# A dense product moved to the loop's end, an unbroken ring of banks, bf16 prefix sums, a 128-row gates' product, and a second DMA issuer for the queries

## The chip, the cores and the metric

One NeuronCore of a Trainium2 chip runs the whole kernel. The metric is the device time of one execution in microseconds. Three runs of the kernel before are shown, and one profiled execution.

## What is computed

Eight batches of 512 tokens with 128 features go through two layers:

```python
x = L0_attn_x                                   # (8, 512, 128)
xn = layernorm(x)
x = x + L0_attn(xn) + L0_ffn(xn)
xn = layernorm(x)
x = x + L1_attn(xn) + L1_ffn(xn)
```

L0_attn is a causal linear attention with Taylor features (16 heads of width 8) beside an attention with a sliding window of 64, both put through Wout. L0_ffn has four layers: `silu(x w1) * (x w2)`, two dense layers h1 and h2 of 512 to 512 with gelu, and w3 of 512 to 128. L1_attn is a causal softmax attention. L1_ffn sends each token to its best 2 of 8 experts: softmax gates of the two best logits, expert e computes `gelu(x W1[e] + b1[e]) W2[e] + b2[e]`, and the results are summed by gate.

## The kernel before, in words

The kernel is written per engine, with an order set out by hand and semaphores between engines. A **batch** goes through four stages on TensorE: `linear_stage` (linear scores of this batch, between them the causal maxima of the previous batch), `causal_stage` (causal scores of the previous batch, sliding maxima of this), `slide_stage` (sliding scores of this batch, projections and the first FFN layer of the next) and `dense_stage` (the FFN's h1 and h2 of the next batch; `mixed_first`, which ends layer 0 of this batch; then the second layernorm, keys k2, queries q2, values v2 and the router's logits of this batch). An opening prepares batch 0, the first batch is written out, batches 1 to 6 run in a loop on every engine (`Fori`, line 898 on TensorE, 1059 on ScalarE, 1613 on VectorE), the last is written out, and a tail finishes its causal attention. Behind the tail, 78 expert tiles are worked through.

**The ring of banks.** Every product that another engine evacuates is a *unit*. `units_of` lists a part's units in TensorE's order, and `PLACE` gives unit n the bank n mod 7. TensorE may begin a unit when its bank's previous unit has been *taken* (`to_bank`, line 521). Each part starts at bank 0 again. The loop's part has 234 units, so its last ones (xnT2, v2, logits) lie in banks 0, 1 and 2, and the first linear products of the next turn follow in the same banks. `first` has 145 units, `last` 213.

**What crosses the joint between two batches.** On TensorE the loop's turn ends with xnT2, v2 and logits. The next turn begins with linear products (six, of which four come before `prefix`), then `h2_3`, four more linear products, `third_layer` (w3), two more, and then the causal maxima, which wait for the second queries (`slots_q2`). `h2_3` is the fourth quarter of the dense layer h2, whose inputs `hidden_b` were ready long before. `prefix` (lines 656 and 659) sums `picks`, the one-hot choices of experts, over the tokens before each: one product with the strict triangle `before_p` and four with `ones`, all fp32. VectorE takes the logits, shifts them (`shift_logits`), takes v2 and then ranks the experts (`choose_experts`) and writes `picks`. In the next turn it places the rows, waits for `third_layer` to add it up in `xs`, and runs through the causal maxima.

**Queues.** ScalarE evacuates k2 and q2 as high parts (`split_hi`), VectorE as low parts (`split_lo`). SyncE (SP) sends them to scratch memory in DRAM (`split_and_send`: two copies of the high part, one of the low part; first k2, then q2) and fetches them back in another layout (`fetch_sent`), with a wait for the complete sends before each fetch. After q2's fetch has landed it fetches q1 of the next batch. ScalarE issues DMAs only at the opening, 21 later loads, b2's among them.

**mixed_causal** (`mix_causal`, lines 631 and 632) ends layer 1's attention: for each of four token tiles `gatesT` (8 rows) times `b2` (8 rows) and, on the same sum, the attention's 128 rows times wo1. Both are fp32, two passes each.

## Time and profile before

| | us |
|---|---|
| median of 3 runs | 1498.56 |
| lowest and highest | 1495.23, 1499.37 |
| the profiled execution | 1501.17 |
| its span, first to last instruction | 1499.3 |
| TensorE busy (share of the span) | 1330.5 (89%) |
| VectorE, ScalarE, GpSimd busy | 817.6, 707.5, 603.3 |
| mean granted TensorE clock | 0.934 |

The span is the stretch in which all rows below lie; 1.9 us of the profiled execution lie around it. In the rows PE is TensorE, PEld its weight loads, DVE VectorE, ACT ScalarE, SP SyncE; a "q" behind an engine's name marks its sequencer or its DMA issues. An fp32 product appears as two passes, so its count is doubled. "Idle before" names what released the engine; "issue" is idle time without a releaser in the trace. PEclk is the granted share of TensorE's full clock.

### The profile page before, as it was taken

How to read it: one execution, taken by the hardware profiler on the slowest of the kernel's cores; microseconds unless marked ns; L12 is line 12 of the kernel's file. 1: busy time of each engine (PE TensorE's matmuls, PEld its weight loads, DVE VectorE, ACT ScalarE, POOL GpSimd, SP SyncE). 2: the span in 40 equal slices, each digit the busy share in tenths (PEclk: the TensorE clock that was granted, in tenths of full speed). 3: DMA queues.
4: the chain of work that ended last, by engine and by line, in shares of the span. 5: the costliest groups of instructions: out<-in, count | busy, mean ns of one | idle time of the engine just before them, and what ended most of it. 6: DMA issues, size and time to landing. Idle time of an engine off the chain costs nothing.

```text
span 1499.3 us, 28932 instructions
## 1 busy us (share of the span) xinstructions
PE 1330.5 (89%) x9122; PEld 917.4 (61%) x9122; DVE 817.6 (55%) x3372; ACT 707.5 (47%) x1511; POOL 603.3 (40%) x791
## 2 busy tenths in 40 slices
PE   5979999989998999989998999899989965679997
PEld 2545567656664666466656665566566743459997
DVE  3064377537753676367635753486357545436654
ACT  2435247524761466246623662366235610437765
POOL 6123334323441334143414342343243435228787
PEclk9988999999999899999998999899999975789999
DMA  9203310331023202330233022402240025014343
GB/s 263 79 2 97 94 58 9 104 101 54 8 84 95 77 9 79 83 95 10 79 76 102 10 79 50 126 11 72 57 123 13 3 70 179 7 31 66 57 65 47
DMA packets 82246, 102.07 MB, mean 68 GB/s; under 512 B 12472, under 2 KB 43104, under 8 KB 82016
## 3 DMA queue, kind: packets, MB, share of 16 engines
q1 hardware_dynamic: 63616, 86.53, 20.9%
q0 software_dynamic: 14304, 10.61, 4.5%
q10 hardware_dynamic: 4176, 3.01, 0.7%
q8 instruction: 84, 1.38, 0.4%
q14 instruction: 66, 0.54, 0.1%
HBM read 55.44 MB, written 46.37 MB: 68 GB/s over the span
## 4 chain that ended last, share of the span: by engine, by line
PE 61%; issue 14%; DVE 11%; POOL 4%; DMA 3%; ACT 2%; SPq 2%; ACTq 1%; another core or an unknown queue 1%; POOLq 0%; DVEq 0%
PE bank L552 16%; PE bank L545 16%; PE heads L609 11%; PE bank L534 6%; PE bank L530 3%; POOL out L1146 3%; DVE hrow L1284 2%; PE bank L649 2%; DVE hT_s L1284 2%; DVE xnT_s L1284 2%; SPq L425 1%; PE bank L539 1%; DVE mx_c L1284 1%; ACT probs L926 1%; ACTq L1049 1%
## 5 line engine op out<-in xcount | busy, mean ns | idle before, releaser
L926 ACT ACTIVATE probs<-bank 128x512 f32<-128x512 f32 (+2 forms) x896 | 442.5, 574 | 421.8 <-PE bank L552 419.2
L552 PE MATMUL bank<-K,Q 128*128 128x192 f32 (+4 forms) x1024 | 237.0, 323 | 37.8 <-DVE mx_c L1284 12.7
L1084 POOL TENSOR_SCALAR_AFFINE_SELECT probs<-probs 128x384 f32<-128x384 f32 x256 | 127.8, 523 | 325.4 <-ACT probs L926 299.7
L552 PE MATMUL bank<-Q,K 128*128 128x192 f32 (+4 forms) x1024 | 216.9, 328 | 16.1 <-DMA Q<-mrow_c 9.8
L552 PEld LDWEIGHTS bank<-K,Q 128*128 128x128 f32 x1024 | 172.3, 197 | 81.1 <-DVE mx_c L1284 35.1
L609 PE MATMUL heads<-probs,V 128*9 128x192 f32 (+4 forms) x3072 | 205.3, 410 | 15.4 <-DVE probs L1333 5.5
L552 PEld LDWEIGHTS bank<-Q,K 128*128 128x128 f32 x1024 | 155.3, 201 | 46.5 <-issue 24.0
L552 PE MATMUL bank<-QM,K 128*128 128x512 f32 (+3 forms) x512 | 141.9, 366 | 29.1 <-issue 18.9
L609 PEld LDWEIGHTS heads<-probs,V 128*9 128x9 f32 x3072 | 77.6, 93 | 132.7 <-issue 90.4
L1146 POOL DMA_INDIRECT out<-h1T_s x78 | 123.3, 1581 | 52.2 <-ACT h1T_s L1038 27.7
L916 ACT ACTIVATE probs<-bank,sh_s 128x512 f32<-128x512 f32 x64 | 44.0, 688 | 202.6 <-PE bank L545 202.6
L545 PE MATMUL bank<-probs,h2T_s 128*128 128x512 f32 x256 | 127.9, 643 | 4.8 <-ACT probs L916 4.8
L552 PEld LDWEIGHTS bank<-QM,K 128*128 128x128 f32 x512 | 87.2, 201 | 54.7 <-issue 24.1
L1030 ACT ACTIVATE h2T_s<-bank,h1T_s 128x128 f32<-128x128 f32 x312 | 89.2, 368 | 60.9 <-PE bank L859 48.0
L545 PE MATMUL bank<-probs,h1T_s 128*128 128x512 f32 x256 | 115.2, 594 | 1.1 <-DVE probs L1452 1.1
L1105 POOL TENSOR_TENSOR rs<-pw,half_neg 128x4 f32<-128x4 f32 x32 | 32.3, 1020 | 203.8 <-DVE pw L1246 203.8
L1097 POOL TENSOR_SCALAR_AFFINE_SELECT probs<-probs 128x512 f32<-128x512 f32 x64 | 54.9, 858 | 141.5 <-ACT probs L926 141.4
L1130 POOL DMA_INDIRECT sorted_rows<-rows,slot_i x64 | 63.6, 993 | 104.8 <-DVE mx_c L1284 86.1
L1313 DVE COPY ot<-heads 128x512 f32<-128x512 f32 x64 | 44.2, 690 | 101.0 <-PE heads L609 101.0
L545 PEld LDWEIGHTS bank<-probs,h2T_s 128*128 128x128 f32 x256 | 52.2, 211 | 61.6 <-issue 60.9
L859 PE MATMUL bank<-h1T_s,w_in 128*128 128x128 f32 x624 | 83.9, 278 | 0.0
L867 PE MATMUL bank<-w_out,h2T_s 128*128 128x128 f32 x624 | 82.5, 275 | 0.3 <-ACT h2T_s L1030 0.3
(188 smaller groups left out, 2090.3 us busy)
## 6 DMA issues: line engine op xcount, KB each, us to landing
Q<-slots_of_q SPq DMA_DIRECT2D x16, 1024.0 KB, 7.9
slots_of_q<-Q SPq DMA_DIRECT2D x48, 256.0 KB, 3.9
K<-slots_of_k SPq DMA_DIRECT2D x64, 192.0 KB
QM<-slots_of_qm SPq DMA_DIRECT2D x8, 1024.0 KB, 9.2
slots_of_k<-QM SPq DMA_DIRECT2D x24, 256.0 KB, 4.1
slots_of_qm<-Q SPq DMA_DIRECT2D x24, 256.0 KB, 4.3
slots_of_k<-Q SPq DMA_DIRECT2D x24, 256.0 KB, 3.0
h1T_s<-sorted_rows SPq DMA_DIRECT2D x78, 65.0 KB
```

The costliest lines, as they stand in the source:

```text
L534: pe.matmul(to_bank(run, unit)[:, :], w, x, start=True, stop=True).then_inc(full_sem(run, unit), 1)
L545: mm = pe.matmul(to[:, :], w[:, k, c * P:(c + 1) * P], src[k], start=(k == 0), stop=(k == FC - 1))
L552: mm = pe.matmul(to[:, at:at + right.shape[1]], left, right, start=True, stop=True, skip_group_check=True)
L609: mm = pe.matmul(heads[ROWS * i:ROWS * i + D + 1, P * j:P * j + widths[j]], V[:, j, HG * g + i, :], slot_of(kind, 2 * g + i // 2)[:, at:at ...
L859: mm = pe.matmul(tile_hidden_bank(i)[:, c * P:(c + 1) * P], w_in[:, i % WB, c * P:(c + 1) * P], tile_xT[:, i % 2, :], start=True, stop=True)
L867: mm = pe.matmul(tile_out_bank(i), tile_hidden[i % 2][:, c * P:(c + 1) * P], w_out[:, i % WB, c * P:(c + 1) * P], start=c == 0, stop=c == ...
L926: return act.activation(to, bank, func, scale=scale, bias=bias).then_inc(taken_sem(run, unit), 1)
L1030: last = act.activation(tile_hidden[i % 2][:, c * P:(c + 1) * P], tile_hidden_bank(i)[:, c * P:(c + 1) * P], ACT.Gelu, bias=tile_b1[:, i % ...
L1084: pool.affine_select(out=three, in_=three, compare_op=ALU.is_ge, fill=0.0, base=0, pattern=[[0, 3], [1, P]], channel_multiplier=-1)
L1130: pool.indirect_dma_start(out=sorted_rows, out_offset=bass.IndirectOffsetOnAxis(ap=slot_i[:, n:n + 1], axis=0), in_=rows[:, n // K2, n % K ...
L1146: pool.indirect_dma_start(out=out.rearrange("b t d -> (b t) d"), out_offset=bass.IndirectOffsetOnAxis(ap=tile_rows[:, i % XB, P + 1:P + 2] ...
L1284: last = dve.tensor_tensor_reduce(beside[:, at:at + n], bank_of(run, unit)[:, at:at + n], mask, 1.0, NEG, ALU.add, ALU.max, mx[:, to:to + 1])
```

## The change

Five things are changed at once. `h2_3` of the next batch is computed at the end of `dense_stage`, behind logits, and no longer in the next linear stage; its gelu is at the end of ScalarE's turn, which then raises a new semaphore `hidden_ready`, and `third_layer` waits for that and comes after the sixth linear product in place of the tenth. `places_of` skips banks at one unit in the middle of a part (h1_1, or cols2 in the last part), so that each part that has one ends on bank 6 and the ring goes on unbroken at its end. `picks`, `before_p` and `ones` become bf16. `gatesT` and `b2` get 128 rows, of which 120 are zero; GpSimd clears both at the start and b2 is loaded as the last of ScalarE's opening loads, after that clearing. q2 is sent by ScalarE's queue, right behind its own high part. Besides, VectorE takes v2 before it takes the logits.

```diff
@@ linear_order
-        units += linear(m) + (["prefix"] if m == 3 and before else []) + (["h2_3"] if m == 5 else []) + (["third_layer"] if m == 9 else [])
+        units += linear(m) + (["prefix"] if m == 3 and before else []) + (["third_layer"] if m == 5 else [])
@@ dense_order
     units += ["hT2", "k2", "q2", "xnT2", "v2", "logits"] if this else []
+    units += ["h2_3"] if after else []
@@
-PLACE = {part: {u: (n % BANKS, n // BANKS) for n, u in enumerate(units)} for part, units in UNITS.items()}
+def places_of(units):
+
+    at, done, place = 0, [0] * BANKS, {}
+    passed = "h1_1" if "h1_1" in units else f"cols{SLIDE}"
+    for unit in units:
+        at += -len(units) % BANKS if unit == passed else 0
+        place[unit] = at % BANKS, done[at % BANKS]
+        done[at % BANKS] += 1
+        at += 1
+    return place
+
+
+PLACE = {part: places_of(units) for part, units in UNITS.items()}
@@ build
-        b1, b2 = sb("b1_s", [P, E * FC]), sb("b2_s", [E, P])
+        b1, b2 = sb("b1_s", [P, E * FC]), sb("b2_s", [P, P])
-        gatesT = sb("gatesT_s", [E, T])
+        gatesT = sb("gatesT_s", [P, T])
-        picks, place = sb("picks", [P, NT + 1, K2 * E]), sb("place", [P, NT, K2 * E])
+        picks, place = sb("picks", [P, NT + 1, K2 * E], BF16), sb("place", [P, NT, K2 * E])
-        before_p, ones = sb("before_p", [P, P]), sb("ones", [P, P])
+        before_p, ones = sb("before_p", [P, P], BF16), sb("ones", [P, P], BF16)
@@ sync: body
                     split_and_send(run, (b, 0), "k2")
-                    split_and_send(run, (b, 0), "q2")
@@ tensor
             def third_layer(run):
-                wait_taken(run, f"h2_{FC - 1}")
+                pe.wait_ge(S["hidden_ready"], due("hidden_ready", (run[1], 0), 1))
@@ tensor: linear_stage
                     if m == 5:
-                        dense(run, "h2_3", h2T, hidden_b, 3)
-                    if m == 9:
                         if not before:
@@ tensor: dense_stage
                     project_rows(run, "logits", xnT, wgT[:, :], E)
+                if after:
+                    dense(run, "h2_3", h2T, hidden_b, 3)
@@ scalar: linear_stage
-                    if n == 5:
-                        gelu(run, "h2_3", hidden_c[3], sh2[:, 3:4])
@@ scalar: dense_stage
                     split_hi(run, now, "q2", bq1[:, 0:1])
+
+                    view = scratch["q2"].rearrange("h (s d) t -> s h d t", d=D)
+                    high, low = parts_of["q2"]
+                    act.wait_ge(S["hi_q2"], due("hi_q2", now, 1))
+                    act.sem_inc(S["unread"], 1)
+                    for s in (0, 1):
+                        act.dma_start(view[s], high.bitcast(F32)).then_inc(S["sent_q2"], 16)
+                    act.wait_ge(taken_sem(run, "q2"), taken_at(run, "q2"))
+                    act.sem_inc(S["unread"], 1)
+                    act.dma_start(view[2], low.bitcast(F32)).then_inc(S["sent_q2"], 16)
                 if after:
                     gelu(run, "h2_2", hidden_c[2], sh2[:, 2:3])
+                    gelu(run, "h2_3", hidden_c[3], sh2[:, 3:4])
+                    act.wait_ge(taken_sem(run, "h2_3"), taken_at(run, "h2_3"))
+                    act.sem_inc(S["hidden_ready"], 1)
@@ scalar: opening loads
+            act.wait_ge(S["cleared"], 1)
+            act.dma_start(b2[0:E, :], dram["b2"]).then_inc(S["later_weights"], 16)
@@ gpsimd
+            pool.memset(b2[:, :], 0.0)
+            pool.memset(gatesT[:, :], 0.0)
             pool.memset(half_neg[:, :], -0.5).then_inc(S["cleared"], 1)
@@ vector
-                take(run, "gatesT", gatesT[:, :], lambda x: x[0:E, :])
+                take(run, "gatesT", gatesT[0:E, :], lambda x: x[0:E, :])
@@ vector: dense_stage
                     take(run, "xnT2", xnT[:, :])
-                    take(run, "logits", lg[:, :, :], lambda x: x[:, 0:NT * E].rearrange("p (t e) -> p t e", e=E))
-                    shift_logits(run, now)
                     dve.wait_ge(full_sem(run, "v2"), full_at(run, "v2"))
...
+                    take(run, "logits", lg[:, :, :], lambda x: x[:, 0:NT * E].rearrange("p (t e) -> p t e", e=E))
+                    shift_logits(run, now)
                     choose_experts(now)
```

## Rows read from the trace of the kernel before

**Rows 1.** The page's busy time, share and instructions of each engine.

```profile
PE 1330.5 (89%) x9122; PEld 917.4 (61%) x9122; DVE 817.6 (55%) x3372; ACT 707.5 (47%) x1511; POOL 603.3 (40%) x791
```

**Rows 2.** Timeline of TensorE: start, us, engine, line, operation, out<-in, shapes, xcount [idle <-releaser].

```profile
481.26 1.06 PE L539 MATMUL bank<-wgT_s,xnT_s 128*128 128x8 f32 x8
486.34 2.17 PE L552 MATMUL bank<-QM,K 128*128 128x512 f32 x6 [4.02 <-issue]
488.31 0.66 PE L656 MATMUL bank<-picks,before_p 128*128 128x80 f32 x2
...
490.41 1.20 PE L552 MATMUL bank<-QM,K 128*128 128x256 f32 x3
491.41 5.87 PE L545 MATMUL bank<-probs,h2T_s 128*128 128x512 f32 x8
...
498.16 3.73 PE L649 MATMUL bank<-w3T_s,probs 128*128 128x128 f32 x32
...
502.20 0.68 PE L552 MATMUL bank<-K,Q 128*128 128x512 f32 x3
```

**Rows 3.** Waits of TensorE, 310 to 960 us: who <- whom: us, times, longest.

```profile
PE bank L552 <- issue: 18.9, 5, 4.0
```

**Rows 4.** Line 898, 470 to 490 us: duration ns min/median/max, first and last start.

```profile
L898 PEldq COMPARE_BRANCH  x1: 4616/4616/4616, 481.4 to 481.4; - x1
```

**Rows 5.** Timeline of VectorE, 470 to 495 us.

```profile
470.70 0.69 DVE L1555 TENSOR_TENSOR x<-bank,xs 128x512 f32<-128x512 f32 x1 [5.30 <-PE bank L641]
...
493.23 0.23 DVE L1360 TENSOR_TENSOR place<-bank,base 128x64 f32<-128x64 f32 x1 [7.29 <-issue]
```

**Rows 6.** Timeline of ScalarE, 479.9 to 481 us.

```profile
480.00 0.69 ACT L916 ACTIVATE probs<-bank,sh_s 128x512 f32<-128x512 f32 x1 [0.17 <-PE bank L545]
```

**Rows 7.** Line 1059 (ScalarE's loop), columns as in rows 4.

```profile
L1059 ACTq FUSED_REGOPS  x1: 50/50/50, 480.3 to 480.3; - x1
```

**Rows 8.** Windows: stretch, its us, busy (instructions) by engine, PEclk, DMA share, GB/s.

```profile
485.80:496.00 10.20, 9.66 (x25) 6.80 (x26) 1.05 (x7) 3.15 (x6) 5.46 (x7) 0.50 0.74 180
```

**Rows 9.** Timeline of TensorE, 0 to 95 us (the opening and the first batch).

```profile
59.31 2.07 PE L552 MATMUL bank<-QM,K 128*128 128x512 f32 x9
61.22 3.60 PE L545 MATMUL bank<-probs,h2T_s 128*128 128x512 f32 x8
```

**Rows 10.** Timeline of TensorE, 330 to 347 us (another joint with a branch).

```profile
331.87 1.97 PE L552 MATMUL bank<-QM,K 128*128 128x512 f32 x6 [4.04 <-issue]
...
346.36 0.68 PE L552 MATMUL bank<-K,Q 128*128 128x512 f32 x3
```

**Rows 11.** Timeline of TensorE, 468 to 471 us (mixed_first).

```profile
468.71 1.95 PE L641 MATMUL bank<-wout_s,attnT 128*128 128x128 f32 x16
```

**Rows 12.** Timeline of TensorE, 176 to 195 us (the loop's entry).

```profile
176.56 1.06 PE L539 MATMUL bank<-wgT_s,xnT_s 128*128 128x8 f32 x8
...
181.29 0.45 PE L656 MATMUL bank<-picks,before_p 128*128 128x80 f32 x2 [1.84 <-DVE picks L1352]
...
194.84 0.45 PE L552 MATMUL bank<-K,Q 128*128 128x512 f32 x1
```

**Rows 13.** Timeline of the SyncE queue, 478 to 496.5 us.

```profile
480.87 1.99 SPq L399 DMA_DIRECT2D slots_of_q<-Q  x3
...
487.19 8.79 SPq L408 DMA_DIRECT2D Q<-slots_of_q  x2
```

**Rows 14.** Windows, columns as in rows 8.

```profile
482.00:484.00 2.00, 0.32 (x3) 0.23 (x3) 1.57 (x6) 0.00 (x0) 0.93 (x1) 1.00 0.94 287
```

**Rows 15.** Timeline of TensorE, 589.3 to 592.9 us (mixed_causal).

```profile
589.45 0.48 PE L631 MATMUL bank<-b_s,gatesT_s 8*128 8x128 f32 x2
589.87 0.49 PE L632 MATMUL bank<-wo_s,attnT 128*128 128x128 f32 x2
```

**Rows 16.** Windows behind a mixed_causal, columns as in rows 8.

```profile
895.00:905.50 10.50, 10.50 (x74) 8.18 (x76) 3.83 (x7) 5.07 (x12) 3.71 (x6) 0.52 0.09 27
```

**Rows 17.** Timeline of the ScalarE queue, 14 to 17.5 us (an opening load).

```profile
14.69 2.38 ACTq L1049 DMA_DIRECT2D earlier_s<-in_earlier  x1
```

More of the change, by code:

```diff
@@ L180 @@
 UNITS = {part: units_of(*has) for part, has in PARTS.items()}
-PLACE = {part: {u: (n % BANKS, n // BANKS) for n, u in enumerate(units)} for part, units in UNITS.items()}
+def places_of(units):
[8 more added lines that the diff above has]
+PLACE = {part: places_of(units) for part, units in UNITS.items()}
 def units_in(part, bank):
-    return len(range(bank, len(UNITS[part]), BANKS))
+    return sum(at == bank for at, _ in PLACE[part].values())
 def units_before(part, bank):
@@ L308, in build @@
             "x1_ready": 1, "shifted": 1, "exped": 1, "gated": 1, "picked": 1, "placed": 1, "rows_filled": 2, "gates_filled": 1,
-            "token_laps": 1, "third_added": 1, "rows_sent": NT * K2 * 16,
+            "token_laps": 1, "hidden_ready": 1, "third_added": 1, "rows_sent": NT * K2 * 16,
             "routing_set": 0, "after_sent": 0, "pads_sent": 0, "pads_counted": 0, "list_laps": 0, "lists_ready": 0,
@@ L1045, in _ @@
                            (bv1[:, :], dram["bv1"].partition_broadcast(P)), (wgT[:, :], dram["wgT"]), (b1[:, :], dram["b1"]),
-                           (bo1[:, :], dram["bo1"].partition_broadcast(P)), (earlier[:, :], dram["earlier"]), (b2[:, :], dram["b2"]),
-                           (wo1[:, :], dram["wo1"])]
+                           (bo1[:, :], dram["bo1"].partition_broadcast(P)), (earlier[:, :], dram["earlier"]), (wo1[:, :], dram["wo1"])]
             for dst, src in later_loads:
                 act.dma_start(dst, src).then_inc(S["later_weights"], 16)
-            assert len(later_loads) == LATER_LOADS
+            act.wait_ge(S["cleared"], 1)
+            act.dma_start(b2[0:E, :], dram["b2"]).then_inc(S["later_weights"], 16)
+            assert len(later_loads) + 1 == LATER_LOADS
             act.wait_ge(S["setup_done"], 1)
```

## The prediction

> **What bounds the kernel now.** I read the page's engine shares first. TensorE is busy for 1330.5 of 1499.3 us [rows 1], so the kernel gets faster where TensorE has less to issue, idles less or runs more often at its upper clock. Next I read TensorE's timeline from one batch to the next. The router's projection (logits) ends at 482.32 (481.26 + 1.06), then TensorE idles 4.02 us and resumes at 486.34 [rows 2]. That idle has no releaser ("issue"); the waits add five of them up to 18.9 us [rows 3]. The sequencer's own row names it: the loop's backward branch begins at 481.4 and takes 4.616 us [rows 4]. Logits had begun only just before it and ran on to 482.32 meanwhile, so queued work goes on under the branch. At the same joint VectorE stands still for 7.29 us with no releaser [rows 5], and ScalarE hardly at all: its last gelu starts at 480.00, and the first register instruction of the next turn is at 480.3 [rows 6, 7]. After the gap TensorE's granted clock is 0.50, that is 1.2 GHz, for 10.2 us [rows 8].
>
> The change touches seven joints between batches: five with a taken branch, and the entry and the exit of the loop, which have none. It also touches the gates' product of each of eight batches, and the last batch's tail. I measure a joint from x1, the residual sum on VectorE (470.70 here [rows 5]), to the first product of the causal maxima, "bank<-K,Q" (502.20 here [rows 2]).
>
> **h2_3 before the branch.** It leaves the lower clock, where it takes 5.87 us [rows 2], and goes behind logits, where it should take the 3.60 us of the upper clock [rows 9]. It lies in the bank of h2_2, so it waits for that gelu, which I put at 482.6 (below): 0.2 us of idle. It starts at 482.55, and what follows could go at 486.0. Like logits it is eight passes, so I let the branch begin as soon as the wait clears: 482.6 + 4.6 + 0.3 = 487.5 against 486.34 before. That is **1.1 us later**, but with h2_3 done, and with 1.4 us of idle instead of 4.0. Behind it, new: six linear products 1.91 us (59.31 to 61.22 [rows 9]), the prefix 0.45, the third layer 3.5 (its row's 3.73 less the overlap with its follower [rows 2]), six linear products more 2.0: **7.85 us** to the causal maxima. Old: 486.34 to 502.20, 15.9 us here. Another such joint takes 331.87 to 346.36, 14.5 [rows 10]; three more are like that one. Net 4 x (14.5 - 7.85 - 1.1) + (15.9 - 7.85 - 1.1) = 22.2 + 6.95 = **29.2 us**. Of this the prefix and the clock are a part.
>
> **Prefix in bf16.** Five fp32 products take ten passes, 488.31 to 490.41, 2.1 us [rows 2] at the lower clock. In bf16 each is one pass. No row has such a pass; the nearest are fp32 passes of 128 columns, 16 in 1.95 us, 0.12 each [rows 11], and double that at the lower clock: five take 0.6 to 1.2 us by them. The prefix has only 240 columns of the 640 in five such passes, which would be 0.22. Between 0.22 and 1.2 I take 0.45, near the rows' upper-clock end. VectorE's writing of picks as bf16 may cost or save a tenth of a microsecond; at a branch nobody waits for it. At the joints without one TensorE waits 1.84 us for picks [rows 12]; h2_3 now covers that.
>
> **Joints without a branch.** Old: logits end at 177.6, maxima at 194.84, 17.2 us [rows 12]. New: 0.2 + 3.45 + 7.85 = 11.5. But the second queries must have landed: their fetch starts at 487.19, and the next one, which waits for them, has been issued at 495.98 [rows 13], so they land at 495.5 or so, x1 + 24.8. With the 0.5 us of the next part this bounds the joint from below at x1 + 24.3. That is 4.5 us won instead of 5.7 at the entry, a little more at the exit: **9.4 us** for both. At a branch my sum gives 495.2, x1 + 24.5: the queries are just in time there, and no more can be had.
>
> **q2 sent by ScalarE's queue.** SP issues the sends from 480.87, behind the keys, 1.99 us for three [rows 13]. ScalarE has finished the high part before its gelu at 480.00 [rows 6], so the first send can go 0.9 us earlier. The DMA engines' share is already 0.94 over 482 to 484 [rows 14], so early queries delay keys: the gain at the fetch is between 0 and 0.9, and lies near the saturated end, 0.5 at most. The price is on ScalarE: three issues of 0.66 (SP's) and two waits ahead of the gelu of h2_2, which moves from 480.00 to 481.9 and is done at 482.6. Queued behind it are h2_3's gelu and ScalarE's branch; TensorE waits 0.2 us for it, counted above. ScalarE is next needed at 488.3. SP passes on to the fetch of the keys, which waits for their landing as before. In the tail, where the maxima wait for the queries alone, **0.5 us** is gained.
>
> **Gates' product over 128 rows.** Pairs of passes of 8 rows and of 128 rows alternate, a pair every 0.42 us (589.45, 589.87), so 3.4 us for 16 passes [rows 15]. Mixed_first is 16 passes of the same size, all of 128 rows, in 1.95 us [rows 11]. Eight times 1.45 is **11.6 us**, on the path since TensorE has no idle around it. The clock fell behind three of these eight: once to 0.52 for 10.5 us, 5 us lost [rows 16], twice for about 3.3 us, 1.6 each. The passes over 8 rows come right before it fell; I credit half of 8.2, **4 us**, with bounds of 0 and 8.2.
> The Trainium skill (TensorE: Matmul & The Clock Gate, "Step-by-step: what each phase is for") says that the time of a weight load goes by its columns and "row count K doesn't matter here". By that rule alone this part would bring nothing; the two rows speak against it.
>
> **Ring, memsets, b2.** The skip now stands at h1_1, which comes onto the last slide products' banks, long read by then: 0 us, and an exponential (0.6 us) where one isn't. In exchange the first linear products no longer follow v2 and logits in their banks. Two memsets and a later load of b2 lie beside the opening's loads: 0 us, bound 1.
>
> **Clock and VectorE.** The clock fell at all seven joints ([rows 8] is one of them), each time after 1.3 to 4 us of idle with small products around it. A dense h2_3 and 1.4 us of idle is better but not clean. I charge half the joints with a short stretch of 3.4 us at half speed: 7 x 0.5 x 1.7 = **-6**. VectorE, back at about 492.6, has placed rows by 493.8; the third layer ends at 494.2. Its refetch under full DMA queues may run late: **-3**.
>
> **Sum.** 29.2 + 9.4 + 0.5 + 11.6 + 4 - 6 - 3 = 45.7. The profiled execution took 1501.17 us (span 1499.3), 2.6 above the median of the three runs: 1501.2 - 45.7 = 1455.5, as a median **1453**.
>
> **Rivals.**
> (a) The branch isn't covered: its refetch begins when the queue is empty. Against it: the branch row began while logits ran. For it: it ended 3.67 us after logits did, which fits as well. TensorE then resumes at 486.0 + 3.67 + 0.35 = 490.0, 2.6 later, and the long idle brings the 7 us stretch back, 2.6 more than charged: 5 x 5.2 = 26, **1479**.
> (b) ScalarE's branch, now behind h2_3's gelu at 487.1, turns as costly as VectorE's 7 us. The third layer's bank then waits for the first square until about 495.0 and the maxima start at 500.6: 5 x 5.4 = 27, **1480**. For it: ScalarE's loop gets some ten instructions longer. Against: ScalarE has 1511 operations in all and hardly a stop, VectorE 3372 and 7 us [rows 1].
> The Trainium skill (Runtime: NRT & Kernel Launch, "Instruction fetch mechanics") says that a taken branch whose target lies outside a window of two pages forces a fetch. The rows agree, and by it (b) needs a body near that limit.
> (c) The 128-row product gains nothing, clock included: 1453 + 15.6 = **1469**.
> (d) Slower: the DMA issues hold ScalarE. One of its opening loads took 2.38 us to issue [rows 17]. With d per issue, each of eight chains (seven with h2_3, one tail) is 3 x (d - 0.66) later; 45.7 + 4.5 is used up at d = 2.75. At 3.3 it is 63 us, **1516**. Against it: SP issues the same shapes in 0.66.
> (e) The clock stays up everywhere: 6 + 4 + 3 better, **1440**.
>
> **How the numbers follow.** The forecast with its smaller variants 0.58, (a) 0.14, (b) 0.06, (c) 0.10, (d) 0.04, (e) 0.05, a mixture that ends within 0.3% of before 0.03. The range takes in (e), (c), (a) and (b): 1439 to 1481; (d) stays out. About 0.3% (4.5 us) is what a measurement of this kernel can tell from no change. Faster 0.93, same 0.03, slower 0.04.
>
> **What would show it.** Right: the branch row begins near 482.6 and TensorE resumes 1 to 2 us after h2_3; near 4 us it is (a). The first square within 1 us of the first linear product rules out (b). Sixteen passes of mixed_causal in 2 us rule out (c). The maxima should start at x1 + 24.5 (31.5 in the joint read here). Wrong would be: queries landing later than x1 + 25, as the new bound, or a clock of 0.50 for 7 us at most joints.

## The result and the profile after

| | before | after |
|---|---|---|
| median | 1498.78 | 1450.01 |
| lowest and highest | 1495.23, 1499.37 | 1449.43, 1454.95 |
| span of the profiled execution | 1499.3 | 1447.7 |
| mean granted TensorE clock | 0.934 | 0.954 |

The ratio of the times is 0.9687, with a 95% interval of 0.9661 to 0.9713: 3.1% less. The forecast was 1453.0 with a range of 1439 to 1481. The total came out close. Single terms of the sum didn't: the joints without a branch and the fifth part brought less than forecast, the clock more.

First the page's engine shares, which answer to [rows 1]: TensorE is busy for 49 us less, in 40 passes less (five in each of eight prefixes), and the other engines do what they did.

```profile
PE 1281.5 (89%) x9082; PEld 883.7 (61%) x9082; DVE 817.4 (56%) x3372; ACT 705.5 (49%) x1511; POOL 604.2 (42%) x793
```

Next TensorE's timeline at the same joint as [rows 2]. Here x1 is at 460.1.

```profile
470.68 1.06 PE L553 MATMUL bank<-wgT_s,xnT_s 128*128 128x8 f32 x8
473.15 5.40 PE L559 MATMUL bank<-probs,h2T_s 128*128 128x512 f32 x8 [1.42 <-ACT probs L930]
477.98 1.56 PE L566 MATMUL bank<-QM,K 128*128 128x512 f32 x6
479.38 0.21 PE L670 MATMUL bank<-picks,before_p 128*128 128x80 bf16 x1
479.42 0.26 PE L673 MATMUL bank<-picks,ones 128*128 128x64 bf16 x4
479.54 0.71 PE L566 MATMUL bank<-QM,K 128*128 128x256 f32 x3
480.44 3.84 PE L663 MATMUL bank<-w3T_s,probs 128*128 128x128 f32 x32 [0.19 <-ACT probs L940]
484.03 1.75 PE L566 MATMUL bank<-QM,K 128*128 128x384 f32 x10
486.06 0.73 PE L566 MATMUL bank<-K,Q 128*128 128x512 f32 x3 [0.28 <-DMA Q<-slots_of_q]
```

The 4 us hole ahead of the linear products is gone. In its place stand 1.42 us ahead of h2_3, ended by ScalarE's gelu, and 0.28 us ahead of the maxima, ended by the queries' landing. The maxima start at x1 + 26.0, where it was x1 + 31.5.

The branch's own row, now line 912, says that it runs under h2_3 (five of them; columns as in [rows 4]):

```profile
L912 PEldq COMPARE_BRANCH  x5: 4006/4188/5287, 326.2 to 910.7; - x5
```

TensorE's waits over 310 to 960 us, as in [rows 3]. The old first row, 18.9 us of "issue" in five holes, has shrunk to 3.4 in two, and two new releasers have come in:

```profile
PE bank L559 <- ACT probs L930: 6.5, 5, 1.6
PE bank L566 <- issue: 3.4, 2, 2.1
...
PE bank L566 <- DMA Q<-slots_of_q: 2.5, 3, 1.3
```

Then the queues that feed this: ScalarE's timeline and its DMA issues (ACTq), from the evacuation of q2 to the gelu of h2_2, which answers to [rows 6]:

```profile
468.55 0.69 ACT L930 ACTIVATE Q<-bank,bq_s 128x512 fp32r<-128x512 f32 x1 [0.17 <-PE bank L548]
469.34 1.31 ACTq L1042 DMA_DIRECT2D slots_of_q<-Q  x2
470.76 1.53 ACTq L1045 DMA_DIRECT2D slots_of_q<-Q  x1
472.41 0.69 ACT L930 ACTIVATE probs<-bank,sh_s 128x512 f32<-128x512 f32 x1 [3.17 <-issue]
```

and SyncE's queue, which answers to [rows 13]. The first fetch of K is issued when all keys have landed, here at x1 + 14.3; the second of the two issues in the last row follows when the queries have landed.

```profile
474.45 2.85 SPq L421 DMA_DIRECT2D K<-slots_of_k  x4
477.42 8.88 SPq L423 DMA_DIRECT2D Q<-slots_of_q  x2
```

VectorE has no hole without a releaser any more, where [rows 5] had 7.29 us. It writes picks in time and then waits for the prefix:

```profile
474.54 0.27 DVE L1381 TENSOR_SCALAR picks<-rank 128x32 bf16<-128x32 f32 x2
479.72 0.22 DVE L1389 TENSOR_TENSOR place<-bank,base 128x64 f32<-128x64 f32 x1 [4.91 <-PE bank L673]
```

Last the clock, in windows of the joint with the columns of [rows 8]: 3.4 us at 0.50, that is 1.2 GHz, against 10.2 us before, and all of it under the branch.

```profile
470.00:474.40 4.40, 2.98 (x18) 2.16 (x17) 3.77 (x11) 0.69 (x1) 1.91 (x1) 1.00 0.99 311
474.40:477.80 3.40, 3.40 (x5) 1.35 (x4) 0.37 (x3) 0.00 (x0) 3.40 (x1) 0.50 0.54 154
```

Split by stretches, the 51.6 us between the two spans are: 27.65 from x1 to the first maxima at seven joints (208.5 before, 180.9 after); 18.7 from there to the next x1, six stretches; 1.9 in the stretch behind the last joint; 4.9 from the last x1 to the end; and 1.6 lost ahead of the first x1. Between 160 and 1095 us the clock stood at its lower level for 72 us before (twelve falls) and for 20.5 us after (six falls, 3.4 us each). That window leaves out one fall of before, at its last joint (6.8 us from 1100.1); from the first x1 to the last it was 88.7 us before and 30.1 after.

### The profile page after: what moved, and what is told of

It reads as the page before. It is cut to its first block and busy times, and to the rows that moved or that the text cites. A ratio compares the mean times of both kernels' runs of the same rounds, so it can differ in the third digit from the quotient of the medians.

```text
span 1447.7 us, 28890 instructions
## 1 busy us (share of the span) xinstructions
PE 1281.5 (89%) x9082; PEld 883.7 (61%) x9082; DVE 817.4 (56%) x3372; ACT 705.5 (49%) x1511; POOL 604.2 (42%) x793
## 3 DMA queue, kind: packets, MB, share of 16 engines
q1 hardware_dynamic: 60160, 80.24, 20.4%
q8 instruction: 84, 1.38, 0.4%
## 5 line engine op out<-in xcount | busy, mean ns | idle before, releaser
L566 PE MATMUL bank<-Q,K 128*128 128x192 f32 (+4 forms) x1024 | 212.4, 324 | 12.9 <-DMA Q<-mrow_c 8.5
L623 PE MATMUL heads<-probs,V 128*9 128x192 f32 (+4 forms) x3072 | 197.4, 398 | 17.7 <-DVE probs L1362 5.9
L566 PEld LDWEIGHTS bank<-Q,K 128*128 128x128 f32 x1024 | 152.2, 197 | 42.2 <-issue 23.7
L566 PE MATMUL bank<-QM,K 128*128 128x512 f32 (+3 forms) x512 | 131.6, 347 | 12.2 <-DVE mx_c L1313 3.9
L559 PE MATMUL bank<-probs,h2T_s 128*128 128x512 f32 x256 | 123.9, 627 | 12.7 <-ACT probs L930 10.4
L566 PEld LDWEIGHTS bank<-QM,K 128*128 128x128 f32 x512 | 81.7, 190 | 37.0 <-DVE mx_c L1313 21.6
L559 PEld LDWEIGHTS bank<-probs,h2T_s 128*128 128x128 f32 x256 | 48.7, 199 | 67.2 <-issue 57.8
```

The lines of the kernel that those rows point to most:

```text
L559: mm = pe.matmul(to[:, :], w[:, k, c * P:(c + 1) * P], src[k], start=(k == 0), stop=(k == FC - 1))
L566: mm = pe.matmul(to[:, at:at + right.shape[1]], left, right, start=True, stop=True, skip_group_check=True)
L623: mm = pe.matmul(heads[ROWS * i:ROWS * i + D + 1, P * j:P * j + widths[j]], V[:, j, HG * g + i, :], slot_of(kind, 2 * g + i // 2)[:, at:at ...
```

## The experiments

All are variants of the kernel after, except where it is said. Joints are measured from x1, as in the prediction; "maxima" is the start of the first causal maximum. The kernel before took 1501.27 us beside a0, e1, e2 and e3, 1499.16 beside e4, e5, e7 and e9, and 1479.88 beside e1b, e6, e10 and e11. So kernels of different groups are compared by their ratios to it, of which 0.001 is 1.5 us.

**a0_after.** The kernel after once more, beside the first group of variants, as their base.

> The changed kernel once more, beside the others on one chip. Every theory: 1448 to 1452 us, ratio to the kernel before 0.967 to 0.970. In the profile: second queries landing at x1 + 25 to 26.3, causal maxima starting at x1 + 25 to 26.5 right behind them, TensorE resuming at x1 + 17.9.

1453.15 us (1446.68 to 1456.48), ratio 0.9678 (0.9650 to 0.9706). Maxima at x1 + 25.1 to 26.4 in the loop's joints. The result repeats. Three of its five low stretches (17.1 us between 160 and 1095) lie at other places than in the first profile, so single falls are not to be reasoned from, only their sum.

**e1_q2_by_sp.** SyncE sends the queries again; all else as after.

```diff
                     split_and_send(run, (b, 0), "k2")
+                    split_and_send(run, (b, 0), "q2")
...
-                    act.wait_ge(S["hi_q2"], due("hi_q2", now, 1))
...
-                    act.dma_start(view[2], low.bitcast(F32)).then_inc(S["sent_q2"], 16)
```

> The changed kernel with its fifth part alone undone: SyncE sends q2 again. Theory A (the part costs time): ScalarE's three issues delay the gelu of h2_2, so h2_3, so the branch (x1 + 13.2 in the changed kernel), and the early queries delay keys and queries alike. Then h2_3 begins at x1 + 11.8, the branch at x1 + 12, TensorE resumes at x1 + 16.5, the queries land at x1 + 24.3 to 24.9 and the maxima start at x1 + 24.5 to 24.9, 1.0 us earlier at each of seven joints and 0.5 us in the tail: 1450 - 8 = 1442 us, 0.5% below the changed kernel. Theory B (my prediction: the part brings about 0.5 us a joint): 1453 to 1455. Theory C (indifferent, the queries land when the DMA engines have moved the data): within 2 us of the changed kernel.

1447.48 us (1445.42 to 1449.51), ratio 0.9650 (0.9627 to 0.9673), 5.7 us below a0_after with intervals that overlap; the stretches are clearer. TensorE's timeline, x1 at 459.5:

```profile
471.03 3.68 PE L560 MATMUL bank<-probs,h2T_s 128*128 128x512 f32 x8
474.87 1.25 PE L567 MATMUL bank<-QM,K 128*128 128x512 f32 x6 [0.16 <-issue]
...
483.70 0.73 PE L567 MATMUL bank<-K,Q 128*128 128x512 f32 x3 [1.74 <-DMA Q<-slots_of_q]
```

h2_3 follows logits at once, the branch is covered whole (0.16 us of idle), and the linear products start at x1 + 15.3 instead of 17.9. SyncE's queue:

```profile
469.71 1.93 SPq L414 DMA_DIRECT2D slots_of_q<-Q  x3
472.19 2.51 SPq L421 DMA_DIRECT2D K<-slots_of_k  x4
475.81 8.13 SPq L423 DMA_DIRECT2D Q<-slots_of_q  x2
```

Keys have landed at x1 + 12.6, 1.7 us before the kernel after has them. Queries land at x1 + 23.9 to 25.4 (25.59 in the tail), against 24.8 to 26.3 (26.03). The seven joints add up to 173.2 us instead of 180.9. But TensorE now stands 1.74 us before the maxima: here it is ready 3.3 us earlier (x1 + 22.4 instead of 25.7) and the maxima start 1.8 us earlier, 1.1 in the mean of the seven joints, because the queries are the last to come. Some of the gain is lost again: the six stretches between the joints took 3.2 us more than in the kernel after, with 23.3 us of lower clock in place of 3.4.

**e2_gates_8rows.** The gates' product over 8 rows again.

```diff
-        b1, b2 = sb("b1_s", [P, E * FC]), sb("b2_s", [P, P])
+        b1, b2 = sb("b1_s", [P, E * FC]), sb("b2_s", [E, P])
...
-        gatesT = sb("gatesT_s", [P, T])
+        gatesT = sb("gatesT_s", [E, T])
...
-            pool.memset(b2[:, :], 0.0)
-            pool.memset(gatesT[:, :], 0.0)
```

> The changed kernel with gatesT and b2 of 8 rows again. My working: 16 passes of mixed_causal take 3.4 us and not 1.9, 8 x 1.45 = 11.6 us, and the clock falls behind some of them, up to 8 us more: 1462 to 1470 us. Rival by the rule that rows do not matter to a weight load: 1450 us, with the passes at 0.12 us each.

1463.29 us (1461.59 to 1474.77), ratio 0.9773 (0.9741 to 0.9806), 10.1 us above a0_after. The steps themselves give 8 x 1.43 = 11.4 (below). Only one fall of the clock came behind a mixed_causal here, at 434.2, so in this kernel the rows' effect on the clock isn't told apart from chance.

**e3_prefix_fp32.** picks, before_p and ones in fp32.

```diff
-        picks, place = sb("picks", [P, NT + 1, K2 * E], BF16), sb("place", [P, NT, K2 * E])
+        picks, place = sb("picks", [P, NT + 1, K2 * E]), sb("place", [P, NT, K2 * E])
...
-        before_p, ones = sb("before_p", [P, P], BF16), sb("ones", [P, P], BF16)
+        before_p, ones = sb("before_p", [P, P]), sb("ones", [P, P])
```

> The changed kernel with picks, before_p and ones in fp32 again. TensorE's prefix takes 1.2 to 1.8 us in place of 0.3 to 0.4. If TensorE's own work sets the start of the maxima: 7 x 1.2 = 8 us, 1458. If the landing of the second queries sets it, as the trace of the changed kernel suggests (TensorE idle 0.3 to 1.9 us there), part of this is hidden: 1451 to 1456.

1455.76 us (1450.92 to 1458.8), ratio 0.9705 (0.9678 to 0.9732): 2.6 above a0_after, not told apart from nothing. Its joints add up to 180.2 us, as after (180.9) and a0_after (180.3). The prefix takes 1.08 us here and 0.15 in the kernel after, but the maxima wait for the queries, so that microsecond is hidden.

**e4_h2_3_back.** h2_3 and its gelu back in the linear stage, the third layer behind the tenth product.

```diff
                     if m == 5:
+                        dense(run, "h2_3", h2T, hidden_b, 3)
+                    if m == 9:
...
-                if after:
-                    dense(run, "h2_3", h2T, hidden_b, 3)
```

> The changed kernel with h2_3, its gelu and third_layer in their old places; ring, bf16 prefix, 128 rows and the sends by ScalarE stay. My working: the branch is uncovered again (TensorE idle about 4 us at five joints, the branch row from x1 + 10.7), h2_3 runs at the lower clock, the clock falls for 7 us or more at the joints, the maxima start at x1 + 28 to 29: 7 x 2.5 to 3.5 us more than the changed kernel, 1468 to 1478. Rival (the branch was not what counted, the second queries set the start of the maxima): 1453 to 1460.

1479.56 us (1473.94 to 1481.94), ratio 0.9859 (0.9826 to 0.9891), some 27 us above a0_after. This is the change's largest part. TensorE's timeline at a joint with a branch, x1 at 469.2:

```profile
479.78 1.06 PE L552 MATMUL bank<-wgT_s,xnT_s 128*128 128x8 f32 x8
484.98 2.18 PE L565 MATMUL bank<-QM,K 128*128 128x512 f32 x6 [4.14 <-issue]
...
488.23 4.38 PE L558 MATMUL bank<-probs,h2T_s 128*128 128x512 f32 x8
```

The hole of 4 us is back, and so are the long falls: 71.6 us at the lower clock between 160 and 1095, as before (72) and unlike after (20.5), though the gates' product has its 128 rows here. So the long falls come back with the old place of h2_3, not with the gates' rows. Whether it is the hole of 4 us that brings them isn't shown: the entry and the exit of the loop, which have no such hole, have a fall of 6.8 us each in this kernel as in before. The joints add up to 201.1 us, 20.2 more than after; the other 7 lie outside them, where the six stretches between the joints had 20.4 us of lower clock against 3.4. The branches took 4.7 to 6.5 us, of which below.

**e6_gates_only.** The kernel before, with nothing but the 128 rows (with the memsets and b2's later load).

```diff
-        b1, b2 = sb("b1_s", [P, E * FC]), sb("b2_s", [E, P])
+        b1, b2 = sb("b1_s", [P, E * FC]), sb("b2_s", [P, P])
...
-        gatesT = sb("gatesT_s", [E, T])
+        gatesT = sb("gatesT_s", [P, T])
...
+            pool.memset(b2[:, :], 0.0)
+            pool.memset(gatesT[:, :], 0.0)
```

> The kernel before with the 128-row gates' product as its only change (gatesT and b2 of 128 rows, the memsets, b2's load last). My working: 16 passes in 1.95 us and not 3.4, 11.6 us less, and a clock that falls less often behind them, 0 to 8 us more: 1481 to 1489, ratio 0.987 to 0.992. e2 against the changed kernel gave 10 us. If the gain needs the other changes: within 3 us of the kernel before.

1463.77 us (1459.45 to 1466.48), ratio 0.9891 (0.987 to 0.9912; before was 1479.88 on this chip): 16.1 us won by this part alone. Of that 11.4 are the steps, which leaves 4.7 for the clock, give or take 3 by the interval. The profiles say where it lies: the joints add up to 208.4 us, as in before, and the six stretches between them took 16.4 us less, of which 8.6 are six steps and 7.8 the clock. Before had three falls behind a mixed_causal (17 us in all), this kernel has none; its falls at the joints are longer in return (10.2 us at five of them, where before had 6.8 at four and 10.2 at one), so that between 160 and 1095 it stood low for 68 us against 72. The sum of the joints hides two shifts: the five with a branch took 1.8 us more, the entry 1.7 less.

**e5_gates_grouped.** 8 rows, but the four gates' products first, then the four of wo1. In this order the result leaves out part of the gates' share of b2 (relative error 0.031), but the passes are the same sixteen, so its time can be read.

```diff
-                    pe.matmul(o, gatesT[:, t * P:(t + 1) * P], b2[:, :], start=True, stop=False)
-                    mm = pe.matmul(o, attnT[:, CAUSAL, t * P:(t + 1) * P], wo1[:, :], start=False, stop=True)
+                    pe.matmul(o, gatesT[:, t * P:(t + 1) * P], b2[:, :], start=True, stop=False, skip_group_check=True)
+                for t in range(NT):
+                    o = to[:, t * P:(t + 1) * P]
+                    mm = pe.matmul(o, attnT[:, CAUSAL, t * P:(t + 1) * P], wo1[:, :], start=False, stop=True, skip_group_check=True)
```

> The changed kernel with gatesT and b2 of 8 rows again, but the four gates' products stand first and the four of wo1 behind them, in place of taking turns. If a change of rows between successive passes is what costs (0.31 us from an 8-row pass to the next of 128 rows against 0.11 between equals): 16 passes in about 2.3 us, 1451 to 1456 us, between the changed kernel and the one with turns. If each pass over 8 rows costs by itself: 3.4 us again, 1462 to 1466. If the clock reacts to 8-row passes, the lower clock appears behind mixed_causal in some batches here as well.

1457.24 us (1452.22 to 1459.76), ratio 0.9716 (0.969 to 0.974), between a0_after and e2_gates_8rows. The step itself decides. TensorE's timeline at the same mixed_causal, first of e2_gates_8rows, whose pairs start 0.41 us apart, 3.15 us from the first to the next product (579.03 to 582.18):

```profile
579.03 0.48 PE L645 MATMUL bank<-b_s,gatesT_s 8*128 8x128 f32 x2
579.44 0.49 PE L646 MATMUL bank<-wo_s,attnT 128*128 128x128 f32 x2
...
582.18 0.67 PE L566 MATMUL bank<-Q,K 128*128 128x192 f32 x4
```

then the kernel after, 0.22 us apart, 1.72 us in all (574.45 to 576.17):

```profile
574.45 0.41 PE L645 MATMUL bank<-b_s,gatesT_s 128*128 128x128 f32 x2
574.69 0.39 PE L646 MATMUL bank<-wo_s,attnT 128*128 128x128 f32 x2
...
576.17 0.67 PE L566 MATMUL bank<-Q,K 128*128 128x192 f32 x4
```

and e5_gates_grouped, 2.00 us in all (576.98 to 578.98):

```profile
576.98 1.15 PE L645 MATMUL bank<-b_s,gatesT_s 8*128 8x128 f32 x8
578.07 1.16 PE L648 MATMUL bank<-wo_s,attnT 128*128 128x128 f32 x8
578.98 0.67 PE L566 MATMUL bank<-Q,K 128*128 128x192 f32 x4
```

Eight passes over 8 rows take what eight over 128 rows take (1.15 and 1.16 us). What costs is the change of rows from one product to the next: (3.15 - 1.72) / 8 = 0.18 us each. The two changes of the grouped order cost 0.28 together by this count, which leaves out the half that stands ahead of the first row; counted from the pass before, they cost 0.37 (2.21 against 1.84 us). The single passes show both halves: the first pass behind a change starts 0.20 us behind its predecessor and the second 0.21, where equal rows give 0.11.

**e7_ring_broken.** Without the skip, so each part starts its ring at bank 0 over whatever lies there.

```diff
-        at += -len(units) % BANKS if unit == passed else 0
```

> The changed kernel with the skip of banks taken out: each part's units lie in banks n mod 7 from 0 again. The third linear product of a turn then lies in h2_3's bank and waits for that gelu, done at x1 + 19.2, so TensorE loses about 0.7 to 1.2 us behind the branch; since the second queries land at x1 + 25 to 26 and TensorE is ready at x1 + 25 to 25.9, 0.3 to 0.8 us a joint is left: 1453 to 1459. Rival (the ring is worth nothing, as I put it): within 2 us of the changed kernel.

1455.59 us (1449.59 to 1456.93), ratio 0.9704 (0.9679 to 0.973), 0.0026 or 3.9 us above a0_after, intervals overlapping. Its joints add up to 179.3 us, 1.6 less than after. The wait that I expected isn't there: the six passes ahead of the prefix take 1.08 us, or 1.38 with the clock down, as in the kernel after (1.10 and 1.40). It had nine falls of the clock against five and six in the two profiles after, 30.7 us against 17.1 and 20.5, which would be 5 to 7 us of work. That the broken ring causes them isn't shown. Inconclusive: the intervals leave the ring anything from nothing to some 9 us.

**e9_q2_by_sp_lead14.** e1_q2_by_sp with fourteen linear products ahead of the maxima instead of twelve, to fill the wait for the queries.

```diff
-LEAD, BEHIND = 12, 8
+LEAD, BEHIND = 14, 8
```

> The changed kernel with q2 sent by SyncE, and LEAD 14 in place of 12: two more linear products stand ahead of the causal maxima. With the sends by SyncE TensorE is ready at x1 + 23.3 and the second queries land at x1 + 24.0 to 25.4. If their landing is the bound of the joint, two linear products (0.7 us) fit into the wait and are worth up to 0.7 us at each of seven joints: 1447.5 - 4 = 1443 to 1445. If TensorE's own work is the bound: 1447.5 within 2 us.

1476.87 us (1474.25 to 1479.28), ratio 0.9855 (0.983 to 0.9879): 0.0205 or 31 us slower than e1_q2_by_sp, a clear miss. At the joint it did what it should, the maxima start at x1 + 24.1 to 25.8 as in e1, with two more products ahead of them. The price lies behind: TensorE's largest waits in e1_q2_by_sp were, from and to the same tiles,

```profile
PE bank L567 <- DVE mx_c L1304: 12.8, 45, 1.3
...
PE heads L624 <- POOL probs L1105: 6.5, 8, 2.1
```

and here

```profile
PE heads L624 <- POOL probs L1105: 22.1, 15, 2.4
...
PE bank L567 <- DVE mx_c L1304: 17.6, 48, 1.6
```

20 us more waiting for VectorE and GpSimd, whose work the linear products had covered, and lower clock in the stretch of the maxima (44.4 us between 160 and 1095, against 27.3). The window 345 to 360 us, in e1_q2_by_sp, where it begins at x1 + 31.0, and then here, where it begins at x1 + 28.2 (at x1 + 31.0 it has 13.14 us of TensorE at the same 0.77):

```profile
345.00:360.00 15.00, 14.09 (x82) 8.04 (x81) 12.90 (x63) 5.98 (x11) 6.59 (x12) 0.90 0.04 14
```

```profile
345.00:360.00 15.00, 11.07 (x62) 5.97 (x63) 9.42 (x44) 3.37 (x6) 7.29 (x13) 0.77 0.14 52
```

TensorE is busy for 1293.6 us against 1281.2 with the same 9082 passes. Filler moved into one wait was taken out of another.

**e11_q2_after_gelu.** ScalarE still sends the queries, but behind the gelu of h2_2, so that it doesn't hold TensorE.

```diff
+                if after:
+                    gelu(run, "h2_2", hidden_c[2], sh2[:, 2:3])
+                if this:
...
                     act.wait_ge(S["hi_q2"], due("hi_q2", now, 1))
...
                     act.dma_start(view[2], low.bitcast(F32)).then_inc(S["sent_q2"], 16)
                 if after:
-                    gelu(run, "h2_2", hidden_c[2], sh2[:, 2:3])
```

> The changed kernel with ScalarE's three issues for q2 moved behind the gelu of h2_2. Theory H (the hold of ScalarE is what the part costs): h2_3 begins at x1 + 11.8 in place of 13.2 and TensorE resumes at x1 + 16.3; the queries leave 0.8 us later. If the hold is the whole cost, 1446 to 1449 like e1. Theory D (the queries sent beside the keys on a second queue delay both, and the landing of the queries is the bound): landing stays at x1 + 25 to 26 and the time at 1451 to 1455, although TensorE resumes earlier.

1433.85 us (1433.04 to 1441.2) beside 1479.88 before, ratio 0.9701 (0.9678 to 0.9724), no better than after. Its TensorE, x1 at 461.1:

```profile
472.62 3.68 PE L559 MATMUL bank<-probs,h2T_s 128*128 128x512 f32 x8
478.01 1.26 PE L566 MATMUL bank<-QM,K 128*128 128x512 f32 x6 [1.72 <-issue]
```

The hold on ScalarE is gone and h2_3 follows logits at once; ScalarE's first send leaves only 0.15 us later than in the kernel after, where I had expected 0.8. But 1.7 us are lost again in the branch, which begins at x1 + 10.8 and takes long:

```profile
L912 PEldq COMPARE_BRANCH  x5: 4520/5671/6413, 326.2 to 913.2; - x5
```

The trace of the DMA queues says why. Under each taken branch of TensorE, in all fourteen profiles, exactly one packet of 16 KB of instructions runs on queue 8, for 0.9 to 1.5 us, and the branch ends 1.3 to 1.7 us behind it; the branch that isn't taken, at the loop's exit, has none and takes 0.08 us. Only the packet's start varies much. With the branch at the same place (x1 + 10.7 to 10.8), it starts 1.4 to 2.4 us behind the branch's own start where SyncE alone sends (before, e6, e1, e1b, e9 and e10) and 2.2 to 4.2 us behind it where ScalarE sends as well (here and in e4). In the longest but one here, the packet comes 3.9 us behind the branch's start at 326.2; the DMA view of 328 to 332 us has its row (queue and kind, packets, MB, share):

```profile
q8 instruction: 1, 0.02, 1.5%
```

The queries land at x1 + 24.7 to 26.2, as in the kernel after, and the joints add up to 180.3 us. So the cost of the fifth part at the joint is not ScalarE's time but that two queues send side by side: it delays the keys, the queries and the branch.

**e1b_q2_by_sp and e10_q2_fetch_in_four.** The first is e1 again as a base on this chip; the second is e1 with the queries' fetch as four DMAs with a semaphore each, where each group of four heads waits for its own.

```diff
+                elif name == "q2":
+                    for g in range(G):
+                        sp.dma_start(to[:, g, :].bitcast(F32), scratch[name].rearrange("(g i) r t -> g (i r) t", i=HG)[g]).then_inc(S[f"slots_q2_{g}"], 16)
...
-                    pe.wait_ge(S["slots_q2"], due("slots_q2", previous, 16))
+                    if before and n % GROUP == 0:
+                        pe.wait_ge(S[f"slots_q2_{n // GROUP}"], due(f"slots_q2_{n // GROUP}", previous, 16))
```

> The kernel of e1 once more (q2 sent by SyncE), as the measure beside e10 and e11 on one chip: ratio to the kernel before 0.963 to 0.967.

> The kernel of e1 with the second queries' fetch cut into four DMAs of 256 KB, one for each group of four heads; the causal maxima wait for their own group's quarter. If the landing of the queries is the bound of the joints, the first quarter lands 3 us or more ahead of the last: the maxima start when TensorE is ready, x1 + 23.3 to 23.6 in place of 24.1 to 25.6, about 1.2 us at each of seven joints, and 2 to 5 us earlier in the tail, where TensorE waits for the queries alone: 10 to 13 us, 1434 to 1438. If the DMA engines serve all four together and they land at one time, or if each more DMA costs its overhead: 1445 to 1449.

e1b: 1430.87 us, ratio 0.9665 (0.9641 to 0.9689). e10: 1416.52 us (1412.18 to 1419.25), ratio **0.9584 (0.9562 to 0.9606)**: 4.2% below before, and below the kernel after and e1b without an overlap of the intervals. Against e1b it won 14.4 us, where I had expected 10 to 13. SyncE's queue and TensorE, x1 at 743.3:

```profile
759.55 2.48 SPq L424 DMA_DIRECT2D Q<-slots_of_q  x4
767.90 0.37 SPq L426 DMA_DIRECT2D Q<-slots_of_q  x1
```

```profile
763.92 1.75 PE L571 MATMUL bank<-QM,K 128*128 128x384 f32 x10
766.41 0.73 PE L571 MATMUL bank<-K,Q 128*128 128x512 f32 x3 [0.74 <-DVE xs L1493]
```

The last quarter has landed at 767.8 (the row at 767.90 waits for it), as late as the whole did; the first landed at x1 + 22.4, and the maxima began 1.4 us ahead of the last. They start at x1 + 22.5 to 24.7, seven joints add up to 163.7 us where e1b has 174.0, and what is last at this joint, as at three others, is VectorE's sum xs and no longer a DMA. The lower clock took only 6.8 us between 160 and 1095. The tail's maxima start at x1 + 23.2 instead of 25.5, and from the last x1 to the end 2.6 us were gained.

## Why the forecast held, and where it didn't

**h2_3 before the branch: right in mechanism, 1.1 us short per joint.** The branch row begins as h2_3 does, and TensorE goes on 0.35 to 0.7 us behind its end, so rival (a) is out. I had the branch at x1 + 11.9 and TensorE back at x1 + 16.8; it was x1 + 13.2 and 17.9. The step that missed is the price of ScalarE's issues: 0.66 each from SP's row gave a gelu at x1 + 11.2. The first measured 0.53 to 0.61 us, the second 0.66 to 0.86, but the third 0.78 to 1.67, and the gelu came at x1 + 12.3. Why the third is slow stays open: it follows a wait, but so does the first. e4_h2_3_back prices the part at 20 us on the joints and 27 in all, against 29.2; part of the 29.2 was the clock, and e4 shows that it was this part that took the long falls away. The five joints with a branch gave 21.2 us together.

**Joints without a branch, and the bound: right that the queries' landing is the floor, wrong on its place.** The sum had them at x1 + 24.3, a half microsecond earlier than before. They came at x1 + 24.8 to 26.3, later than in the kernel before (24.2 to 24.9), and at each of the seven joints the maxima follow the landing by 0.1 to 0.6 us. The text named this as what would be wrong, "queries landing later than x1 + 25, as the new bound": it happened at five joints of seven. The entry gave 2.6 us and the exit 3.9, 6.5 where the sum had 9.4 (its own numbers give 9.0: at the exit the bound leaves 4.5, not more than at the entry). Joints gave 27.65 us net where the sum had 29.6 (29.2 + 9.4 less the 6 and the 3).

**q2 by ScalarE: wrong in sign.** The sum had +0.5 with bounds of 0 and 0.9 at the fetch. I had written that early queries delay keys, and yet left a loss out. The keys landed at x1 + 14.3 to 15.2 in place of 12.6 to 13.3, so K's fetch began 1.7 us later. The queries' sends did land earlier, but SyncE issues the fetch of K first, and only behind it that of Q: Q's fetch was issued at x1 + 16.7 in the mean of seven joints, 0.3 later than in e1, and then took 8.9 us instead of 8.1, with K's fetch beside it. Where it was issued at x1 + 16.1 at a joint with a branch, it landed at x1 + 26.2 and 26.3, where before and e1 have 23.9 to 24.8 from about the same start; at the exit it landed at 24.8 against 24.1. e1_q2_by_sp brings both landings back and takes 7.7 us off the joints; e11_q2_after_gelu shows that the hold of ScalarE alone isn't the cost. In the whole kernel's time e1's 5.7 us lie within the overlap of the intervals; the stretches and landings show the loss. The DMA share over the four microseconds of sending is 0.94 in the kernel after and 0.92 in e1 and in before: there was no free share for a second issuer to fill. The windows of the kernel after and of e1:

```profile
469.40:473.40 4.00, 2.58 (x21) 2.33 (x20) 3.44 (x9) 0.69 (x1) 0.91 (x1) 1.00 0.94 278
```

```profile
468.80:472.80 4.00, 4.00 (x25) 2.91 (x23) 3.44 (x9) 0.69 (x1) 0.87 (x1) 1.00 0.92 283
```

The Trainium skill (Trainium Kernel Development and Optimization, "Key Constraints") says that DMAs of all queues run on the same 16 engines and that issuing from several saves issue time alone. These runs agree and go further: here it cost the keys 1.7 us and the queries 1.

**Prefix in bf16: right, and smaller.** From the start of the first of the five passes to that of their follower it is 0.16 us (479.38 to 479.54), below my lower bound of 0.22, where I took 0.45. At the joints it earned next to nothing, because the queries are last (e3_prefix_fp32).

**Gates over 128 rows: right to a hundredth.** 1.43 us per step where the sum had 1.45; rival (c) is out. e6_gates_only gave 16 us against 11.6 + 4. For the clock, the kernel after has no fall behind a mixed_causal. The rule of the Trainium skill that I weighed, that the row count doesn't matter to a weight load (TensorE: Matmul & The Clock Gate, "Step-by-step: what each phase is for"), holds inside a run of equal products (1.15 and 1.16 us in e5_gates_grouped) and gives no price for a change of rows. I had read [rows 15] as the price of 8 rows; it is the price of alternating.

**Clock: the charge was right in number and wrong in cost.** Four of seven joints had a fall of 3.4 us, the half that I had charged: the entry and three with a branch. At those three the fall lies under the branch, where TensorE has little to lose: at 326, with the clock up, h2_3 took 3.70 us and 2.06 of idle followed; at 473, with the clock down, it took 5.40 and none followed, and both resumed at x1 + 17.9 to 18.1. By the branch's end alone the three could have resumed 0.2 to 0.4 us earlier, and their third layer ended at x1 + 24.1 to 24.3 instead of 23.6. At the entry, which has no branch to hide it, the linear products came at x1 + 18.1, at the exit, with the clock up, at 15.5 (0.8 us of that is its earlier gelu). The queries were later than all of this but once: at one joint the maxima came 0.3 us later than the landing allowed. So of the 6 us hardly any was paid. More came back outside the joints than the 4 that I credited: over the six stretches from the first maxima to the next x1, before had 27.3 us of low clock and the kernel after 3.4. At half speed that is 12 us of work; with six steps of 1.43 it makes 20.6, and these stretches gave 18.7. Stretches without a fall took 121.2 to 121.4 us before and 119.8 to 120.0 after, which is the step alone, so the rest is the clock. Three of the six falls of before stood 36 us behind x1, not behind a mixed_causal, where I had credited nothing.

**VectorE: -3 was not needed.** It came back in time (above). Rivals (b) and (d) are out too: ScalarE's first square starts 0.52 us behind its last gelu, and no issue of ScalarE in the loop took over 1.67 us, where (d) needed 2.75. The sign that I had named for (b), the first square within 1 us of the first linear product, fails by its letter at the four joints with the clock down (1.6 to 1.8 us), since the gelu of a slower h2_3 stands ahead; at the other three it is 0.5 or, at one, 1.5.

**Ring, memsets, b2.** The stretch ahead of the first x1 grew by 1.6 us, where I had 0 with a bound of 1. The memsets and b2's load aren't the cause: alone (e6_gates_only) they put the first x1 at 166.6 against 166.0, and without the memsets (e2_gates_8rows) it came at 169.0. With the other parts it lies anywhere from 166.6 (e4_h2_3_back) to 170.9 (e3_prefix_fp32), so the 1.6 may be no more than scatter. What the ring is worth stays open (e7_ring_broken).

**The sum, term by term**, forecast and then measured: joints 29.6 and 27.65; gates 11.6 and 11.4; the clock outside the joints 4 and 10.1 (18.7 less six steps of 1.43); the opening 0 and -1.6; the last batch and the tail beyond their two gates' steps 0.5 and 3.9, which I didn't take apart. That is 45.7 and 51.5 between the spans (48.8 between the medians). The closeness is luck in part: the fifth part cost the joints 7.7 us, which the clock gave back.

## What to carry to other kernels

Put ready work of about the length of the stall right ahead of a taken branch, on the engine that matters, and look what its first wait is: a wait ahead of it moves the branch as well. Before a second queue sends beside the first, read the DMA share over those microseconds; at 0.92 to 0.94 here, the second only delayed what the first had to deliver, and the branch's instructions too. When a landing is the last thing at a joint, let the consumer wait for its part of it, and count what filler you take from the stretch behind before you move it ahead.

## What the runs showed of the hardware that I had not expected

- A change of the row count from one fp32 product to the next costs 0.18 to 0.19 us, half ahead of its first pass and half ahead of its second; the rows' number itself costs nothing (8 rows: 1.15 us for eight passes, 128 rows: 1.16).
- TensorE's taken branch isn't of one length, and what varies is the start of one packet of instructions. All 70 branches in the fourteen profiles end 1.3 to 1.7 us behind a packet of 16 KB on queue 8. The branch took 4.0 to 5.3 us in the kernel after, where it begins at x1 + 12.4 to 13.3, and 4.5 to 6.5 us in e11_q2_after_gelu and e4_h2_3_back, where it begins at x1 + 10.7 to 10.8 while both queues send, so that an earlier start was lost in it. In e1_q2_by_sp, with one queue sending, it took 4.2 to 4.8 us, and TensorE was back at x1 + 15.3 to 15.9.
- Sends from two queues at once made the last of the first queue's three transfers land 1.7 us later and the second's 0.3 to 1.3 us earlier than one queue did (x1 + 15.5 to 15.9 against 15.9 to 16.9), at a DMA share that stayed between 0.92 and 0.94.
- Four DMAs of a quarter each, issued in a row, landed one after the other, the first three some 0.65 us apart, and the last as late as the one large DMA (x1 + 24.6 in the mean in e10_q2_fetch_in_four and in e1b_q2_by_sp).
- A fall of TensorE's clock of 3.4 us under a branch delayed its next product by 0.2 to 0.4 us and the end of the third layer by 0.5, and the wait for the queries hid that at two joints of three.
